# Expert rows renumbered in DRAM, and their sum over the choices taken with an identity matrix

## What is computed

```python
y = einsum('te,teh->th', combine, expert_out)        # layer 0: 2 experts of each token are not zero
routed = einsum('tef,efd,te->td', act, wd, combine)  # layer 1: 6 experts of each token are not zero
x = x + gb * y                                       # gb: one gate row of 256 values for each sequence
```

## Time and profile before

| what | value |
|---|---|
| median of 3 runs | 2514.99 us (2511.31 to 2516.11) |
| the profiled execution's own time | 2512.04 us |
| its span in the trace | 2510.2 us |
| mean granted TensorE clock | 0.882 of full speed |
| busy: PE, DVE, ACT, POOL | 1960.5, 1673.6, 1452.5, 901.4 us |
| sum of layer 0 (first read issued to the last addition's end) | 834.70 to 855.89 us |
| sum of layer 1 | 2456.77 to 2506.73 us |
| from there to the span's end (last store) | 3.5 us |

### The profile page before, as it was taken

One profiled execution on the slowest core, in us unless ns is written; L12 is line 12 of the kernel. 1 busy time (PEld: TensorE's weight loads), 2 busy tenths in 40 slices (PEclk: granted clock), 3 DMA queues, 4 the chain that ended last, 5 costly groups with the idle time before them and its releaser, 6 DMA issues.

```text
span 2510.2 us, 45756 instructions
## 1 busy us (share of the span) xinstructions
PE 1960.5 (78%) x12107; PEld 1604.7 (64%) x12107; DVE 1673.6 (67%) x3630; ACT 1452.5 (58%) x3953; POOL 901.4 (36%) x832
## 2 busy tenths in 40 slices
PE   4786868687469256999999999999999976049990
PEld 4565656566357245888878887888788864037770
DVE  5666756566324567888888888888888867023445
ACT  1563717364124155888878887888888851025550
POOL 0110203021343110444444444444444434755550
PEclk8897968798589677999999999999999988579995
DMA  3160573022333402444434443444344434234557
GB/s 121 51 184 18 185 200 117 18 84 87 156 100 108 137 5 85 140 150 147 147 124 147 150 149 124 143 150 150 126 143 148 150 98 129 101 114 146 155 156 247
DMA packets 168211, 319.51 MB, mean 127 GB/s; under 512 B 20176, under 2 KB 110288, under 8 KB 165776
## 3 DMA queue, kind: packets, MB, share of 16 engines
q1 hardware_dynamic: 153584, 278.31, 34.8%
q0 software_dynamic: 14496, 39.73, 4.4%
HBM read 231.68 MB, written 86.29 MB: 127 GB/s over the span
## 4 chain that ended last, share of the span: by engine, by line
PE 56%; DVE 13%; ACT 10%; issue 8%; POOL 5%; DMA 4%; PEldq 1%; DVEq 1%; ACTq 1%; PEld 1%; SPq 1%; POOLq 0%
PE bank L1741 13%; PE bank L1795 7%; PE bank L1014 5%; PE bank L1769 5%; POOL sorted_rows L1127 5%; ACT work L669 4%; PE bank L1043 3%; PE bank L1788 3%; PE bank L1781 3%; PE bank L1755 3%; DVE nmax L589 2%; PE bank L1764 2%; PE bank L998 1%; PE bank L741 1%; PEldq L142 1%
## 5 line engine op out<-in xcount | busy, mean ns | idle before, releaser
L1741 PE MATMUL bank<-h_hi,wi 128*128 128x512 f32 x1024 | 402.5, 434 | 1.0 <-ACTq L142 1.0
L1903 DVE SCALAR_TENSOR_TENSOR cv<-bank,cw,cv 128x511 f32<-128x511 f32 (+2 forms) x384 | 287.5, 749 | 84.7 <-ACT cv L1836 49.7
L1830 ACT ACTIVATE l_mat<-l_mat,cum_tok 128x128 f32<-128x128 f32 x1024 | 315.7, 429 | 0.0
L1222 DVE SCALAR_TENSOR_TENSOR experts_sg<-experts_th,bank 128x96 f32<-128x96 f32 (+2 forms) x190 | 53.8, 283 | 331.0 <-ACT experts_th L1092 330.9
L1955 POOL TENSOR_TENSOR xdec<-xdt,dec_tok 128x384 f32<-128x384 f32 x128 | 107.8, 842 | 463.7 <-DVE xdt L1893 463.7
L1970 POOL TENSOR_TENSOR yg<-yd,sgt 128x512 f32<-128x512 f32 x128 | 228.1, 1782 | 77.4 <-DVE yd L1910 77.4
L1795 PE MATMUL bank<-wo,yg 128*128 128x256 f32 x1024 | 242.4, 380 | 0.3 <-POOL yg L1970 0.3
L1131 POOL DMA_INDIRECT chosen_rows<-experts_yo,experts_xt x174 | 167.7, 964 | 191.4 <-ACT experts_yo L1099 187.5
L1741 PEld LDWEIGHTS bank<-h_hi,wi 128*128 128x128 f32 x1024 | 194.5, 190 | 62.4 <-issue 24.4
L1741 PE MATMUL bank<-h_lo,wi 128*128 128x512 f32 x512 | 202.6, 396 | 0.0
L1795 PEld LDWEIGHTS bank<-wo,yg 128*128 128x128 f32 x1024 | 184.8, 190 | 20.6 <-POOL yg L1970 0.7
(11 more groups left out here) (293 smaller groups left out, 4888.1 us busy)
## 6 DMA issues: line engine op xcount, KB each, us to landing
wi<-in_weights_split SPq DMA_DIRECT2D x128, 512.0 KB, 3.5
l_mat<-running_sums SPq DMA_DIRECT2D x128, 512.0 KB, 4.5
experts_xt<-sorted_rows SPq DMA_DIRECT2D x174, 129.0 KB, 2.1
experts_got<-chosen_rows SPq DMA_DIRECT2D x32, 512.0 KB, 8.0
wo<-out_weights_normed SPq DMA_DIRECT2D x128, 128.0 KB, 2.0
sorted_rows<-blank SPq DMA_DIRECT2D x5, 2709.0 KB, 26.6
w_raw<-in_wi SPq DMA_DIRECT2D x32, 256.0 KB, 2.6
in_weights_split<-w_hi SPq DMA_DIRECT2D x32, 256.0 KB, 2.8
```

The source lines that it names most:

```text
L1741: mm = e.matmul(dst[:, :], l, r[:, k, tok], start=(n == 0), stop=(n == 3 * KD - 1))
L1830: last = e.activation(part, part, ACT.Relu, bias=cum_tok[:, c, hh, bass.ds(w.g, 1)], scale=-1.0)
L1903: e.scalar_tensor_tensor(out=cv[:, w.two, n:SEQ], in0=PSX[w.two][:, 0:SEQ - n], scalar=cw[:, bass.ds(w.f, 1), TAPS - 1 - n], in1=cv[:, w.t ...
```

## The change

The row numbers in `chosen_rows` are changed, so that the four rows of one partition, group and choice follow each other: the number is ((b * 128 + p) * 6 + j) * 4 + i for tile i of group b. A read of one block then takes from each partition one piece of 4 KB, and the pieces of neighbouring partitions are 24 KB apart. This holds in both layers (in layer 0 only two of the six places are used). The addition over the choices moves from DVE to PE: for each half of a group (two token tiles, 512 columns) TOP products of the identity with `got` add up in one PSUM bank, 2 * TOP products a group. Two pairs of banks take turns. DVE multiplies the two banks by the gate row into `xn` and adds `xn` to x. SP's wait for a free buffer in layer 1 is on the new signal `s_summed` of PE instead of `s_comb`.

```diff
@@ -932,11 +933,11 @@
             for b in range(GROUPS):
                 if b >= KEPT:
-                    e.wait_ge(*s_comb(b - KEPT + 1))
+                    e.wait_ge(*s_summed(b - KEPT + 1))
+                group = slice(b * TOP1 * SEQ, (b + 1) * TOP1 * SEQ)
                 for j in range(TOP):
-                    first = j * TOKENS + b * SEQ
-                    e.dma_start(got[:, b % KEPT, j, :, :], chosen[layer][first:first + SEQ, :]
-                                .rearrange("(i p) d -> p i d", p=P)).then_inc(s_got[b].sem, 16)
+                    e.dma_start(got[:, b % KEPT, j, :, :], chosen[layer][group, :]
+                                .rearrange("(p j i) d -> p j i d", p=P, j=TOP1)[:, j, :, :]).then_inc(s_got[b].sem, 16)
@@ -1053,6 +1054,18 @@
+            for b in range(GROUPS):
+                e.wait_ge(*s_got[b](16 * TOP))
+                if b == 0:
+                    e.wait_ge(*s_yo(Q))
+                if b >= 2:
+                    e.wait_ge(*s_comb(b - 1))
+                for half in range(2):
+                    for j in range(TOP):
+                        mm = e.matmul(bank[2 * (b % 2) + half][:, :], ident[:, :],
+                                      got[:, b % KEPT, j, 2 * half:2 * half + 2, :].rearrange("p i d -> p (i d)"),
+                                      start=(j == 0), stop=(j == TOP - 1))
+                mm.then_inc(s_summed.sem, 1)
             t.together()
@@ -1254,13 +1267,14 @@
             for b in range(GROUPS):
-                e.wait_ge(*s_got[b](16 * TOP))
-                total = got[:, b % KEPT, 0, :, :]
-                for j in range(1, TOP):
-                    v.step(e.tensor_tensor(total, total, got[:, b % KEPT, j, :, :], ALU.add))
-                v.step(e.tensor_tensor(total, total, gates[:, gate, b:b + 1, :].broadcast_to([P, TT, D]), ALU.mult))
+                e.wait_ge(*s_summed(b + 1))
+                for half in range(2):
+                    v.own.add(e.tensor_tensor(xn[:, 2 * half:2 * half + 2, :],
+                                              bank[2 * (b % 2) + half][:, :].rearrange("p (i d) -> p i d", i=2),
+                                              gates[:, gate, b:b + 1, :].broadcast_to([P, 2, D]), ALU.mult))
+                e.wait_ge(s_dve, v.own.now())
                 rows_b = x[:, b * TT:(b + 1) * TT, :]
-                v.step(e.tensor_tensor(rows_b, rows_b, total, ALU.add))
+                v.step(e.tensor_tensor(rows_b, rows_b, xn[:, :, :], ALU.add))
@@ -2080,8 +2094,9 @@
-    o["tok"] = (np.arange(TOP1)[None, :, None] * TOKENS + np.arange(NT)[None, None, :] * P +
-                part[:, None, None]).astype(np.int32)
+    tiles = np.arange(NT)
+    o["tok"] = (((tiles // TT)[None, None, :] * P + part[:, None, None]) * TOP1 * TT +
+                np.arange(TOP1)[None, :, None] * TT + (tiles % TT)[None, None, :]).astype(np.int32)
```

More of the change, by code:

```diff
@@ L909, in experts @@
         s_comb = signal("combined", GROUPS)
+        s_summed = signal("summed", GROUPS)
         B_T, B_G, B_A, B_Y = (bank[0], bank[1]), (bank[2], bank[3]), (bank[4], bank[5]), (bank[6], bank[7])
```

## The result

The changed kernel takes 2524.73 us (median of 6 runs, 2521.28 to 2531.78) against 2512.38 us (6 runs, 2510.12 to 2516.11) for the kernel before on the same chip. The ratio is 1.0048, with a 95% interval of 1.0032 to 1.0063: about half a per cent slower, 12.3 us. The profiled execution's span is 2522.9 us, 12.7 more than before.

The account below looks back on a forecast made before the run. DMA and DVE were taken to set the pace in turn; PE's 10.32 us a layer 1 group replaces DVE's 8.8. Layer 1 +6.3 and layer 0 +2.0 give 8.3, added to 2515.0: 2523.3 us, range 2516 to 2531.

Parts of the forecast that it names:

- Larger pieces: Reads before the sums: 4 KB pieces move 414 GB/s against 349, so a layer 1 group takes 7.60 us, not 9.01.
- rival 2: Reads of the sums: the rate stays at 349 GB/s, +9.1 us in layer 1, +2.4 in layer 0, 2526.5 us; chance 0.16.
- The product: PE's float32 identity products of 512 columns: 0.86 us each, 10.32 us a group in layer 1, 3.44 in layer 0.
- Rival 1: PE's products cost only 0.89 ns a column, as in turning tiles, so DMA sets the pace: 2504.7 us; chance 0.06.
- DVE behind PE: DVE's two products, addition, wait and PE's drain: 2.94 us a group, hidden beside PE except in the last group.
- The cold PE: PE starts each sum at half clock for 3.0 to 4.1 us, losing 1.8 us once in each layer.
- Rival 3: PE's clock stays at 0.50 through the sums: products cost 1.72 us, 2575 us in all; chance 0.04.
- The first group: First group's data ready at 2466.92 us in layer 1 (was 2468.33) and 839.35 in layer 0.
- The release of a buffer: Layer 1, from a buffer's release to its new data: 10.4 us instead of 11.75, a tie with PE for group 2.
- The scatters: Scatters before the sums keep 1 KB pieces at new addresses: no effect taken, 2.7 us either way for a tenth.
- Two of the signs: Expected: no PE wait over 0.5 us between layer 1's groups, and loops before the sums ending at 2454 and 832 us.
- a sign against itself: The forecast is wrong if the loops before the sums end at other times than 2454 and 832 us.

Follow-up runs that it names:

- PE alone without a pause: Full change with one signal per block, so PE adds each block as it lands and frees its buffer; ratio 1.0010 to the kernel before.
- long row of zeros: Full change plus 36 (layer 0) and 58 (layer 1) PE products of zeros ahead of the sum; ratio 1.0044 to the kernel before.
- short row: Full change plus 24 (layer 0) and 36 (layer 1) PE products of zeros ahead of the sum; ratio 1.0040 to the kernel before.
- stores late: Full change with the first three groups' stores held until group 2 is complete, ratio 1.0045 to before; the same on the layout alone, 0.9991.

## Why the prediction was right, point by point

The forecast was 2523.3 us, 0.33% slower; 2524.7 us and 0.48% were measured. Direction and mechanism held; the loss of 12.3 us was about half as large again as the 8.3 us forecast. That the two times agree within 1.4 us is partly luck: the kernel before came out at 2512.4 us over six runs, 2.6 less than the 2515.0 of the three runs to which the 8.3 us had been added, and this took back most of the 4.0 us that the loss was too small.

- **Larger pieces.** The forecast was 414 GB/s from the earlier trace rows; the windows of the first burst show 393 to 422. Pieces 24 KB apart are read at about the rate of the earlier trace rows, so rival 2 is out. By the rule of the Trainium skill ("DMA: Bandwidth & Descriptors", section on where 436 GB/s comes from) the HBM side would have bound at about 358 GB/s; the reads of this kernel, which has one core at work, were faster, so the traces disagree.
- **The product.** The forecast of 0.86 us from the earlier trace rows was right: 48 products less the cold start take 41.3 us, with two records each. Rival 1, the price of turning, is out. That this is the price of the change is shown by adding two choices of six (58.9 to 41.6 us) and by PE alone without a pause (50.2 us, expected 50.8). Products in the rounded float32 type, which show one record each, were not tried.
- **DVE behind PE.** Its product was forecast at 0.69 us and measured at 0.686; it lies beside PE in all groups but the last, where it ends 2.6 us after PE's last record. With PE's drain of 0.25 us, which the forecast had put into its 2.94, that is 2.84.
- **The cold PE.** This term was too small. Two starts in the trace of before gave 3.0 and 4.1 us at half rate, and 1.8 us lost a layer; it was 5.0 us in layer 0 and 4.7 in layer 1, so 2.5 and 2.4 lost, together 1.3 us more than forecast. Rival 3, a PE that stays cold, is out.
- **The first group.** Data came 5.16 us after the first issue in layer 0 (forecast 4.65) and 10.43 in layer 1 (10.15), together 0.8 us more.
- **The release of a buffer.** This is the largest miss. The forecast was 10.4 us; it was 10.5 for group 2 and 12.1 for group 3. PE waited 0.2 and 1.4 us where a tie was forecast, and since it drains for 0.25 us ahead of each wait, groups 2 and 3 began 0.5 and 1.6 us later than PE alone would have let them, 2.0 us more than forecast, which had 0.1 for group 2. The forecast let both releases cost the same, as they do in the earlier trace rows; why they don't here is the open point above.
- **The scatters.** They were taken at nothing. The tile loop took 225.6 to 230.2 us with the new row numbers and 227.5 and 231.2 with the old ones (the runs on the slower chip left out), so no effect of the addresses can be told.

The mis-sized terms give 1.3 + 0.8 + 2.0 = 4.1 us, less 0.2 at the two ends and 0.1 in the products: with the 8.3 forecast that is 12.1 for the 12.0 of the two sums, the rest being rounding; 0.7 of the spans' 12.7 are other stages.

Two of the signs that the prediction named did not come out as written. PE waited 1.4 us before group 3, where no wait of over 0.5 was to be seen. And the first reads were issued 2.6 and 3.7 us later than before, which the prediction counts as a sign against itself. By the marks above that is no effect of the change on the loops: layer 0's tile loop took 127.7 us in both kernels, and layer 1's was 3.3 us shorter.

## What to carry to other kernels

Before work is moved to an idle engine, price it there per unit of the stage's pace: a float32 identity product of 512 columns at 0.86 us takes 1.7 us for a block that DVE adds in 1.25 us, so the idle engine was the slower one in layer 1, with its six blocks a group. And ask what else the busy engine waits for: here both pipelines waited for whole groups of 3 MB, and signalling and freeing each block by itself gave 8 us in layer 1's sum (49.7 to 41.6, both with the new layout) without moving any work. A better transfer pays only where the transfer binds: the same layout was worth 0.2, 1.6, 1.7 and 4.7 us of that sum in four versions of it.

## What the hardware showed that was not expected

- PE's clock rose only 4.7 and 5.0 us after PE had begun to work without a pause on 512-column float32 products, where two other starts in the trace of before took 3.0 and 4.1 us.
- The clock can fall after the work has begun: in layer 1 of the kernel with the long row of zeros PE had idled 3.09 us, started at 2487.62 at 1.00 and was at 0.50 from 2487.9 to 2491.3. In layer 0 with the short row it had idled 2.97 us, and the clock fell 1.2 us after the start.
- Reads in 4 KB pieces, 24 KB apart in DRAM, move 393 to 422 GB/s in 2 us windows with the DMA share at the top, those in 1 KB pieces 346 to 350, on one core. Counted from the release of their buffer, the last group's reads took 0.9 to 2 us longer than those of the group before in six traces with whole groups (the full change, its stores late, its long row of zeros, the layout only, the same with stores late, and, with 1 KB pieces, the sum on PE only), with stores beside them or without.
